# The future of a causal attention hidden by GpSimd in the exponentials, instead of by mask matmuls on the scores

## What is computed

```python
scores = jnp.einsum('bqhd,bkhd->bhqk', Q, Kp) / jnp.sqrt(jnp.float32(HD))
if causal:
    mask = jnp.tril(jnp.ones((Sq, Sk), bool))
    scores = jnp.where(mask, scores, -jnp.inf)
a = jax.nn.softmax(scores, axis=-1)
o = jnp.einsum('bhqk,bkhd->bqhd', a, V).reshape(Bq, Sq, Dm)
```

## Time and profile before

| | |
|---|---|
| median of three runs | 3578.2 us |
| the profiled execution's own time | 3593.65 us |
| its span, first to last instruction | 3591.9 us |
| TensorE matmul busy | 3051.4 us, 85% |
| VectorE busy | 2111.3 us, 59% |
| ScalarE busy | 1893.7 us, 53% |
| GpSimd busy | 1593.6 us, 44% |
| mean granted TensorE clock | 0.919 of full speed |

### The profile page before, as it was taken

The page is one execution under the profiler, slowest core; times in us unless marked ns, Lnnn a source line. Parts: engine busy times, 40 slices in busy tenths (PEclk is TensorE's granted clock), DMA queues, the critical chain, the costliest instruction groups (busy, mean ns, idle before and its releaser), DMA issues. The chain is left out here.

```text
span 3591.9 us, 54697 instructions
## 1 busy us (share of the span) xinstructions
PE 3051.4 (85%) x18207; PEld 1719.0 (48%) x18207; DVE 2111.3 (59%) x4295; ACT 1893.7 (53%) x3859; POOL 1593.6 (44%) x2792
## 2 busy tenths in 40 slices
PE   6888999898899989899998989888885399999960
PEld 3435444443544454354444435443425177777850
DVE  4877887786788778678877867854352000000016
ACT  4665767567576766757675675735341032223210
POOL 5655554582565467257546725642301500000026
PEclk9999999999999999999999999988985599999985
DMA  3005221541422143042204313132303345455523
GB/s 86 16 27 109 57 65 30 115 95 30 99 61 54 30 92 71 28 83 58 56 28 92 70 29 84 40 75 54 55 9 116 134 147 170 159 171 172 175 73 114
DMA packets 270054, 290.11 MB, mean 81 GB/s; under 512 B 32056, under 2 KB 255680, under 8 KB 269808
## 3 DMA queue, kind: packets, MB, share of 16 engines
q1 hardware_dynamic: 261936, 270.21, 30.0%
q0 software_dynamic: 6144, 16.79, 1.4%
q10 hardware_dynamic: 1728, 0.01, 0.0%
HBM read 224.34 MB, written 62.39 MB: 80 GB/s over the span
## 5 line engine op out<-in xcount | busy, mean ns | idle before, releaser
L1250 ACT ACTIVATE probs<-ps,nbias,sc 128x512 f32<-128x512 f32 x1024 | 790.4, 778 | 275.5 <-DVE nbias L1131 216.9
L997 POOL TENSOR_SCALAR pq<-probs,rstep 128x512 f16<-128x512 f32 x1024 | 709.7, 693 | 252.0 <-PE ps L1364 168.4
L1148 DVE TENSOR_REDUCE m<-ps 128x1 f32<-128x512 f32 (+3 forms) x1024 | 561.1, 583 | 294.0 <-PE ps L1390 150.8
L1128 DVE TENSOR_REDUCE nmax<-ps 128x2 f32<-128x1024 f32 x512 | 620.8, 1212 | 95.4 <-PE ps L1356 94.8
L1387 PE MATMUL ps<-kst,qst 96*128 96x512 bf16 (+3 forms) x1024 | 331.4, 355 | 90.5 <-issue 50.7
L1140 DVE TENSOR_SCALAR big<-ps 128x1024 bf16<-128x1024 f16 x512 | 348.1, 680 | 63.1 <-PE ps L1364 61.4
L1364 PE MATMUL ps<-id,pq 128*128 128x128 f16 x4096 | 330.5, 226 | 47.5 <-DVE big L1140 41.3
L1875 DVE COPY yb<-moe_ps 128x256 f32<-128x256 f32 x78 | 33.1, 425 | 569.5 <-PE moe_ps L1725 569.5
L1409 PE MATMUL ps<-qst,kst 108*128 108x512 bf16 (+3 forms) x1024 | 306.3, 353 | 65.2 <-ACT big L1269 29.9
L1629 POOL DMA_INDIRECT got<-rows_out,slot_of x64 | 69.5, 1085 | 643.1 <-DMA rows_out<-yb 624.5
L1364 PEld LDWEIGHTS ps<-id,pq 128*128 128x128 f16 x4096 | 261.5, 101 | 192.1 <-issue 129.3
(11 more groups left out here) (205 smaller groups left out, 4621.7 us busy)
## 6 DMA issues: line engine op xcount, KB each, us to landing
e_w<-in_L_xattn_e_w_dram SPq DMA_DIRECT2D x78, 1024.0 KB
wring<-in_L_xattn_ff_w_dram SPq DMA_DIRECT2D x96, 256.0 KB, 2.9
parts<-parts_sb SPq DMA_DIRECT2D x64, 384.0 KB, 3.0
kst<-parts SPq DMA_DIRECT2D x192, 128.0 KB, 4.8
qst<-parts SPq DMA_DIRECT2D x192, 128.0 KB, 5.1
moe_in<-rows_in SPq DMA_DIRECT2D x39, 256.0 KB
rows_out<-yb SPq DMA_DIRECT2D x39, 256.0 KB, 2.2
rows_in<-zero SPq DMA_DIRECT2D x19, 512.0 KB, 4.0
```

The costliest lines, as they stand in the source:

```text
L997: nc.gpsimd.tensor_scalar(pq[:, u % 2, h, :], probs[:, u % 2, h, :], rstep[:, u % 2, h:h + 1], HALF_ROUND, ALU.mult, ALU.add).then_inc(SIG ...
L1128: nc.vector.tensor_reduce(nmax[:, n % 2, :], ps[:, a:a + 2, :], AX.X, ALU.max, negate=True).then_inc(SIG["M"], 1)
L1148: nc.vector.tensor_reduce(m32[:, g % 2, t, h:h + 1], bank(("A", B, s, n))[:, 0:width], AX.X, ALU.max, negate=True).then_inc(SIG["am"], 1)
L1250: nc.scalar.activation(probs[:, u % 2, h, :], ps[:, BANKS[("S", B, s, u)][h], :], ACT.Exp, bias=nbias[:, u % 2, h:h + 1], scale=sc[:, s:s ...
```

## The change

The mask matmul of B and its tile `hide_future_t` go. A new step `hf` on GpSimd sets the future of the diagonal 128x128 tile of four heads to zero in `ex`, in one affine select of 128x4x128, after the last E2 of the half; AV2 of the causal stage waits for hf of its key tile. Masking in A stays. The planner's costs follow: hf is entered at 0.8 us and B of the causal stage gets shorter.

```diff
-       "POOL": "Q ms n2 rs xn gb bi spk spq",
+       "POOL": "hf Q ms n2 rs xn gb bi spk spq",
...
-            return 0.22 if s == 4 else 0.06 + 0.055 * (NT - 2 * p - js[0])
-        return 0.43 if s == 4 else (0.5, 0.29)[p]
+            return 0.22 if s == 4 else 0.01 + 0.053 * (NT - 2 * p - js[0])
+        return 0.43 if s == 4 else (0.39, 0.18)[p]
...
-                step("AV2", B, s, n, ("E2", B, s, last_b(g, j // 2)), ("dV", B, s, 1), n and ("AV2", B, s, n - 1),
+                if s == 3:
+                    step("hf", B, s, n, ("E2", B, s, last_b(g, j // 2)))
+                step("AV2", B, s, n, ("hf", B, s, n) if s == 3 else ("E2", B, s, last_b(g, j // 2)), ("dV", B, s, 1), n and ("AV2", B, s, n - 1),
...
-            nc.gpsimd.memset(hide_future_t[:, :], 0.0).then_inc(s_set, 1)
...
-            nc.gpsimd.affine_select(out=hide_future_t[:, :], in_=hide_future_t[:, :], compare_op=ALU.is_ge, fill=MASKED,
-                                    base=0, pattern=[[1, P]], channel_multiplier=-1).then_inc(s_set, 1)
...
+                if kind == "hf":
+                    g, jt = n // NT, n % NT
+                    p, j, i0 = jt // 2, jt % 2, lo(s, jt)
+                    after(pool, "E2", B, s, last_b(g, p))
+                    diagonal = ex[:, ex_half(g, p), :, j, i0:i0 + P]
+                    nc.gpsimd.affine_select(out=diagonal, in_=diagonal, compare_op=ALU.is_ge, fill=0.0,
+                                            base=0, pattern=[[0, HG], [1, P]], channel_multiplier=-1).then_inc(SIG["hf"], 1)
...
-                                                qst[0:rows_, head, i0:N], start=True, stop=not causal(s))
-                        if causal(s):
-                            last = nc.tensor.matmul(dst[:, i0:i0 + P], idb[:, :], hide_future_t[:, :], start=False, stop=True)
+                                                qst[0:rows_, head, i0:N], start=True, stop=True)
...
-                    if j == 0:
+                    if causal(s):
+                        after(pe, "hf", B, s, n)
+                    elif j == 0:
                         after(pe, "E2", B, s, last_b(g, p))
```

More of the change, by code:

```diff
@@ L84 @@
          "dy": 0.6, "g": 0.88, "dg": 0.62, "ge": 6.4, "w": 0.9, "dw": 0.65, "z": 0.97, "dz": 0.6,
-         "bi": 0.7, "gb": 1.53, "ST": 0.5, "LX": 0.5, "LC": 0.5, "st": 0.88, "rs": 1.4, "xn": 0.53}
+         "bi": 0.7, "hf": 0.8, "gb": 1.53, "ST": 0.5, "LX": 0.5, "LC": 0.5, "st": 0.88, "rs": 1.4, "xn": 0.53}
 TAIL = {"PE": 0.13, "DVE": 0.08, "ACT": 0.08, "POOL": 0.0, "SP": 0.0}
@@ L656, in transformer @@
         hide_future = sb("hide_future", [P, P], BF16)
-        hide_future_t = sb("hide_future_t", [P, P], BF16)
         head_row = sb("head_row", [P, 8], F32)
@@ L796, in transformer @@
         NREST = (len(col_names) - len(FIRST_COLS)) * KT + 1 + 2 * 2 * HG
-        CONSTS = 20
+        CONSTS = 18
         ROWS_PER = BLOCKS * BLOCK // P
@@ L927, in _ @@
             nc.gpsimd.memset(v_f32[:, :, :], 0.0).then_inc(s_set, 1)
-            pool.wait_ge(s_set, 9)
+            pool.wait_ge(s_set, 8)
             nc.gpsimd.affine_select(out=id32[:, :], in_=id32[:, :], compare_op=ALU.not_equal, fill=1.0,
@@ L939, in _ @@
                                     base=0, pattern=[[-DH, 8]], channel_multiplier=1).then_inc(s_set, 1)
-            pool.wait_ge(s_set, 14)
+            pool.wait_ge(s_set, 12)
             nc.gpsimd.affine_select(out=head_row[:, :], in_=head_row[:, :], compare_op=ALU.is_ge, fill=0.0,
@@ L1032, in _ @@
         def _(dve):
-            dve.wait_ge(s_set, 15)
+            dve.wait_ge(s_set, 13)
             nc.vector.tensor_copy(id16[:, :], id32[:, :])
@@ L1043, in _ @@
             nc.vector.tensor_tensor(sc[:, 2:4], steps[:, :, 2], steps[:, :, 3], ALU.mult).then_inc(s_set, 1)
-            dve.wait_ge(s_set, 18)
+            dve.wait_ge(s_set, 16)
             nc.vector.tensor_scalar(sc[:, 0:2], sc[:, 0:2], SCALE, None, ALU.mult).then_inc(s_set, 2)
```

## The result

The changed kernel takes 3590.1 us (median of 17 runs, 3584.23 to 3594.32), the kernel before 3579.5 us on the same chip (17 runs, 3574.11 to 3590.09). The ratio is 1.0029, with a 95% interval of 1.0021 to 1.0036: slower by 7.5 to 13 us, where 12.9 us and 3591 us were forecast. The profiled execution of the change took 3592.68 us, that of the kernel before 3593.65 us. Both lie above their medians, the one of before by 0.4%. So a difference of a few us in all is read from the timed ratios, and the traces say where work stands and what waits for what. They can still place the loss: the experts' first instruction (GpSimd's memset of `moe_id`) starts at 2704.4 us before and at 2714.7 now, 10.3 us later.

What follows compares the result with a forecast made beforehand. TensorE and GpSimd were taken to limit the causal stage in turn, the change relieving the first and loading the second. -29.2 + 22.4 + 19.7 = +12.9 us, forecast median 3591 us, range 3556 to 3612.

Steps and rivals of the forecast that it cites:

- The masks that go: TensorE, causal stages: 512 mask matmuls leave at 57 ns each in the stream, -29.2 us.
- The fillers that come: TensorE: the new order holds 841 filler matmuls instead of 737, 104 at 0.215 us each, +22.4 us.
- The selects: GpSimd: 128 affine selects of 128x4x128 float32 at 0.615 us each, in all 79 us, 9.8 per batch.
- Their exposed part: GpSimd's back-to-back stretch: the last head group's four selects a batch are uncovered, 19.7 us in all, bounds 13.8 to 37.0.
- What moves: End of causal stage: the last n2 stands behind 11.5 Q units instead of 9, delaying n3; costed at nothing.
- the case without slack: Start of the cross stage: if no slack absorbs the later n3, y and norm, 4.6 us a batch.
- The wait on the stacked rows: Before a stage's first matmul: the wait of 6 to 10 us on the stacked rows' loads stays.
- ScalarE and the setup: Exponentials' shorter waits for masks (bound 29 us) and the second mask's memset and select (0.14, 0.25 us): zero.
- The batch longer by 1.6 us: Sign in the new profile: batch period, from one stage's first score matmul to the next batch's, longer by 1.6 us.
- TensorE as the real limit: Rival: TensorE's relief counts and selects hide; up to -29.2 us, 3549, more likely -20, 3558; chance 0.20.
- the third rival: GpSimd's line blocked at its head by selects awaiting E2; decides above 0.3 us mean wait; +37 us, about 3615; chance 0.10.
- "The two cancel": Rival: gaps and slack in GpSimd's stretch absorb half of the 19.7 us; -7 to +6, about 3581; chance 0.27.

Runs made afterwards that it cites:

- 3: Kernel before with its 512 mask matmuls left out, own order and 737 fillers kept, no selects: 3577.2 us, ratio 0.9988.
- 1: The changed kernel's order with the computation of the kernel before: masks stay, no selects, 841 fillers: 3611.7 us, ratio 1.0083.
- 2: The changed kernel's order and fillers with neither masks nor selects, so the future is not hidden there: 3589.4 us, ratio 1.0019.
- 5: The changed kernel with every eighth filler matmul not issued, 736 left of 841: 3594.1 us, ratio 1.0040.
- 4: The changed kernel's order, with the last head group hidden by mask matmuls again (96 selects, 128 masks): 3591.2 us, ratio 1.0026.
- 6: The changed kernel with each of its 128 selects issued twice, in the same order: 3629.3 us, ratio 1.0154.
- 9: Kernel before in its own order, masks out, 128 selects put in behind the last E2 of each half with no room planned: 3629.0 us, ratio 1.0140.
- 10: The changed kernel with the select entered in the planner at 0.63 us instead of 0.8, new order, 788 fillers: 3573.2 us, ratio 0.9984.

## Why the prediction came true, step by step

The direction and the size were right, 10 us for 12.9. The working was not: three terms of the sum were each wrong by 16 to 25 us, most of the loss came from a step that I had costed at nothing, and the four errors cancelled. The number came true by luck.

- **The masks that go, -29.2 us.** The mis-sized term. In the order of before they were worth 4 us (3). I had taken TensorE's stream as the limit because its busy share was 94% in the first window. A busy share says how long records stand, not who sets the pace: with the masks gone, TensorE's waits for VectorE grew by a few us and its granted clock fell (0.91 to 0.79 in the stretch shown), which may have taken back a part of the 25 us that are missing. The same masks cost 23 us in the order of the change (1 against 2), in which the planner had left no time for them. So a price per mask exists only together with an order. Why it is five times as high there wasn't tried by itself.
- **The fillers that come, +22.4 us.** Wrong: 105 fewer gave +4 us instead of -22 (5). I had argued in the same passage that a filler stands only where TensorE idles, and still charged it.
- **The selects, 0.615 us each.** Measured 0.634. The 79 us were 78.5 by the group's busy time; GpSimd as a whole grew by 83.1, and kernel 2, with this order and no selects, is already 15 us over before.
- **Their exposed part, +19.7 us.** Wrong as a place and as a size. 4 us (error 5) for all 128 (the change against 2), and none of it with the last group's four (4). The second window is as full as I read it, but what the selects pushed out of it cost little: n2 comes 10.3 us after n1 in the change and in kernel 2, with and without selects (batch 2). That more work on GpSimd can cost most of its length was right, as 6 and 9 show: 45 and 54 us for 83 and 78 us more that was not planned.
- **What moves, nothing.** The step that failed. The order alone gave +11 us (2 against 3). I had named 4.6 us a batch for the case without slack. n3 came 4.8 us later in batch 2 and 8.7 in batch 3, and 1.7 and 3.6 us were still there at the cross stage; over batches 2 to 5 the part from n1 to the cross stage took 12.5 us more. I saw the place and took the slack on trust from a row of fillers; it covered some two thirds.
- **The wait on the stacked rows stays.** Right: 9.06 and 6.74 us, for 9.85 and 6.44.
- **ScalarE and the setup, zero.** Nothing speaks against it. The waits of E2 for the end of B were 138.6 us before (96.6 for the mask, 42.0 for the matmul itself) and are 112.4 now (L1414): 26 us less, near the bound of 29, and the kernel is no faster for it.
- **The batch longer by 1.6 us.** 1.9 in batch 2, 2.7 on the mean of batches 2 to 5.
- **Rivals.** TensorE as the real limit would have given 20 to 29 us in 3, and 4 came; with the lower clock there it isn't refuted outright. The stand before the selects passed the third rival's own mark (0.41 us) without its price. "The two cancel" is nearest to the mechanism: removed and added work are both almost free here, and what is left is the order.

The sum in measured terms: masks -4 (3), the new order +11 (2 against 3), fillers 0, selects +4 (the change against 2), in all +11, and +10 was timed. That it closes proves nothing, as each step starts from the kernel in which the one before ended; taken the other way round, the order costs 30 us with masks in (1) and leaving them out then gives 23.

So the change is slower by its order, not because a select costs more than a mask: the same work in the order of 10 is 16 us faster than the change and 6 faster than the kernel before. The traces place the loss between the last n1 and the cross stage, in the change and in kernel 2 alike, so neither masks nor selects make it. The rows point at the last n2 behind two and a half more Q units and at the 4.1 us block of the split ahead of it, but moving these alone wasn't tried. Kernel 10 has that loss too and makes up for it ahead of n1.

## What to carry to other kernels

Where a scheduler writes the order, a change to its costs is a redraw of the whole order. Here orders of like work lay 0.15 to 0.45% apart, and the edit moved the time by 0.29%; time a few orders of both sides before judging the edit, enter the new operation at its measured time, and run the new order without the new work as a control. Price removed work by leaving it out at a fixed order, not by busy share; don't charge fillers that are put into waits, and compare the granted clock of the two kernels before reading a time difference as a price. Work added to GpSimd's line cost little where room was made for it (4 us for 78.5 us of selects) and most of its length where none was (54 us).

## What was unexpected of the hardware

An affine select of 128 partitions by 4x128 float32 on GpSimd takes 634 ns (628 to 646 in 128 executions), 0.06 us less than its quantising product of the same 512 elements (693 ns on the mean) and a little over half of its two-input subtraction (1156 ns); with 292 ns for 128 elements, 384 more cost 0.34 us. TensorE with 105 filler matmuls fewer kept its granted clock (0.924 for 0.925) and its time, while without the 512 masks, in the order of before, its mean clock was 0.918 for 0.922; over all kernels the clock doesn't rank the times (0.926 in the change, 0.922 in the faster kernel before). And the waits in a profile did not rank the kernels: the fastest one waits three times as long for its selects as the change does, and kernel 10 five times.
